# Denominators' token count moved to ScalarE, unit 14's last two sums moved to VectorE, and new orders on all queues

## What is computed

```python
h = layernorm(x)
q, k, v, g = h @ Wq.T, h @ Wk.T, h @ Wv.T, h @ Wg.T       # q, k turned by rotary sin and cos
kv, ksum, vsum = sum_s k v, sum_s k, sum_s v              # per head
num = q kv * scale + vsum
den = q ksum * scale + seq_len                            # seq_len = 256 tokens
x = x + ((num / den + conv(v, lepe_w, lepe_b)) * g) @ Wo.T
y = (fp8(layernorm(x) / s_in) @ fp8(kernel / s_k)) * (s_in * s_k)
out = x + (bf16(y) + bias)
```

## Time and profile before

| | |
|---|---|
| median of three runs | 168.14 us |
| the profiled execution | 168.33 us |
| its span, first to last instruction | 166.5 us |
| mean granted TensorE clock | 0.975 of full speed |
| PE busy | 151.4 us (91%) |
| DVE busy | 149.5 us (90%) |
| ACT busy | 125.9 us (76%) |
| POOL busy | 136.1 us (82%) |

### The profile page before, as it was taken

One profiled execution on the slowest core, in us unless ns is written; L12 is line 12 of the kernel. 1 busy time (PEld: TensorE's weight loads), 2 busy tenths in 40 slices (PEclk: granted clock), 3 DMA queues, 4 the chain that ended last, 5 costly groups with the idle time before them and its releaser, 6 DMA issues.

```text
span 166.5 us, 3690 instructions
## 1 busy us (share of the span) xinstructions
PE 151.4 (91%) x1052; PEld 123.3 (74%) x1052; DVE 149.5 (90%) x281; ACT 125.9 (76%) x342; POOL 136.1 (82%) x164
## 2 busy tenths in 40 slices
PE   7687999999999999999999999999999999987520
PEld 2365898796877889797988888879979787865300
DVE  1269999999899999999999999999999999999563
ACT  3748857566888888989989898798687977672851
POOL 1426986866899999999989899999879989889860
PEclk9999999999999999999999999999999999999955
DMA  4955030222061915065625536263405131514223
GB/s 128 286 145 136 0 67 2 58 43 63 10 150 32 246 27 140 5 150 137 162 65 129 155 95 194 35 159 85 108 7 122 36 74 23 128 33 99 77 61 112
DMA packets 29286, 15.74 MB, mean 95 GB/s; under 512 B 9680, under 2 KB 26960, under 8 KB 29264
## 3 DMA queue, kind: packets, MB, share of 16 engines
q1 hardware_dynamic: 28688, 15.22, 36.8%
q10 hardware_dynamic: 576, 0.26, 0.6%
HBM read 5.25 MB, written 4.19 MB: 57 GB/s over the span
## 4 chain that ended last, share of the span: by engine, by line
PE 78%; DVE 5%; POOL 5%; issue 4%; SPq 3%; DMA 3%; ACT 1%; POOLq 0%; DVEq 0%; ACTq 0%
PE bank L1284 9%; PE bank L1275 8%; PE p_num L1331 8%; PE bank L1294 8%; PE bank L1320 8%; PE p_num L1339 8%; PE bank L1358 7%; PE bank L1302 7%; PE bank L1310 4%; PE bank L1348 4%; PE bank L1267 4%; DMA w_raw<-in_L_attn_Wo_dram 3%; DVE acc L982 2%; PE bank L1400 2%; POOL yc L724 1%
## 5 line engine op out<-in xcount | busy, mean ns | idle before, releaser
L982 DVE SCALAR_TENSOR_TENSOR acc<-bank,conv_w,acc 128x510 f32<-128x510 f32 (+1 forms) x48 | 34.6, 721 | 0.4 <-ACT acc L433 0.2
L394 ACT ACTIVATE h<-xs,nmr,rs 128x128 f32<-128x128 f32 x64 | 26.2, 481 | 1.2 <-POOL nmr L664 1.2
L452 ACT ACTIVATE h<-x,nmr,rs 128x128 bf16<-128x128 f32 x60 | 24.6, 483 | 2.1 <-POOL nmr L675 1.5
L708 POOL TENSOR_TENSOR k<-k_turned 128x512 f32<-128x512 f32 x16 | 20.4, 1274 | 4.2 <-DVE k_turned L967 4.2
L661 POOL TENSOR_TENSOR rs<-ve,minus_half 128x4 f32<-128x4 f32 (+1 forms) x17 | 16.6, 977 | 8.2 <-ACT ve L385 8.2
L717 POOL TENSOR_TENSOR acc<-acc,outer 128x508 f32<-128x508 f32 x16 | 20.3, 1270 | 1.1 <-DVE acc L982 1.1
L672 POOL TENSOR_TENSOR rs<-ve,minus_half 128x4 f32<-128x4 f32 (+1 forms) x17 | 16.6, 975 | 5.7 <-ACT ve L443 5.7
L701 POOL TENSOR_TENSOR qT<-q_turned,q_swapped 128x512 f32<-128x512 f32 x16 | 20.4, 1274 | 0.6 <-DMA q_swapped<-q_turned 0.6
L967 DVE TENSOR_TENSOR k_turned<-bank,turn_k 128x1024 f32<-128x1024 f32 x16 | 19.5, 1222 | 0.8 <-PE bank L1284 0.6
L955 DVE TENSOR_TENSOR q_turned<-bank,turn_q 128x1024 f32<-128x1024 f32 x16 | 19.4, 1214 | 0.0
L1320 PEld LDWEIGHTS bank<-v,k 128*128 128x128 f32 x128 | 16.5, 190 | 3.5 <-issue 3.3
(11 more groups left out here) (90 smaller groups left out, 338.1 us busy)
## 6 DMA issues: line engine op xcount, KB each, us to landing
q_swapped<-q_turned SPq DMA_DIRECT2D x32, 128.0 KB, 2.4
xs<-_attn_hidden_states_dram SPq DMA_DIRECT2D x15, 256.0 KB, 3.7
out_dram<-ob SPq DMA_DIRECT2D x15, 256.0 KB, 2.7
xs<-_attn_hidden_states_dram SPq DMA_DIRECT2D x2, 128.0 KB, 2.7
turn_q<-in_turn_q_dram SPq DMA_DIRECT2D x1, 256.0 KB, 4.0
turn_k<-in_turn_k_dram SPq DMA_DIRECT2D x1, 256.0 KB, 4.3
out_dram<-ob SPq DMA_DIRECT2D x2, 128.0 KB, 1.8
h2T<-h SPq DMA_TRANSPOSE x14, 2.5
```

The source lines that it names most:

```text
L394: last = nc.scalar.activation(h[:, s, t], xs[:, u % NX, t], ACT.Identity, scale=rs1[:, s, t:t + 1], bias=nmr1[:, s, t:t + 1])
L452: last = nc.scalar.activation(h2[:, s3, t], x2[:, u % 4, t], ACT.Identity, scale=rs2[:, s, t:t + 1], bias=nmr2[:, s, t:t + 1])
L708: nc.gpsimd.tensor_tensor(k[:, u % 3], k_turned[:, s, :, :, 0:D // 2], k_turned[:, s, :, :, D // 2:D], ALU.add).then_inc(k_done, 1)
L982: nc.vector.scalar_tensor_tensor(out=part, in0=p_vT[:, :, lo + off:hi + off], scalar=conv_w[:, k:k + 1], in1=part, op0=ALU.mult, op1=ALU.a ...
```

## The change

The addition of the token count to the denominators becomes an activation on ACT (add_tokens, with the count as a bias held in a new tile `tokens`) for units 0 to 14; den gets a second slot; DVE's invert is the reciprocal alone and waits for den. Unit 15 keeps its additions on DVE, in halves. add_bias(14) and final_sum(14) leave POOL and are done by DVE around end_norm2, with semaphores of their own. The PSUM results are placed in other banks, and the call lists of SP, ACT, POOL, DVE and PE are written in a new order throughout, with waits to match the banks. No step of the computation is left out. Cut to its core (loops, start and end of the lists):

```diff
-        den = sb("den", [P, TPU, H])
+        den = sb("den", [P, 2, TPU, H])
+        tokens = sb("tokens", [P, 1])
...
-        p_q = bank[3]
-        p_k = bank[0][:].rearrange("p (t d) -> p t d", t=TPU)
-        p_v = bank[0][:].rearrange("p (t d) -> p t d", t=TPU)
-        p_kv = bank[2][:, 0:BPU * NW].rearrange("p (j e) -> p j e", j=BPU)
-        p_h2T = bank[3][:, 0:W // 2].bitcast(BF16)
-        p_hT = bank[3]
-        p_proj = bank[1][:].rearrange("p (t d) -> p t d", t=TPU)
+        p_q = bank[4]
+        p_k = bank[3][:].rearrange("p (t d) -> p t d", t=TPU)
+        p_v = bank[2][:].rearrange("p (t d) -> p t d", t=TPU)
+        p_kv = bank[4][:, 0:BPU * NW].rearrange("p (j e) -> p j e", j=BPU)
+        p_h2T = bank[2][:, 0:W // 2].bitcast(BF16)
+        p_hT = bank[2]
+        p_proj = bank[5][:].rearrange("p (t d) -> p t d", t=TPU)
         p_gT = bank[1]
-        p_vT = bank[5][:].rearrange("p (j s) -> p j s", j=BPU)
-        p_t1T = bank[4]
-        p_y = bank[0]
-        p_first_hT = [b[:, 0:S] for b in (bank[5], bank[3])]
-        p_end_h2T = [b[:, 0:S // 2].bitcast(BF16) for b in (bank[0], bank[1])]
-        p_end_y = [b[:, 0:S].rearrange("p (t d) -> p t d", t=TPB) for b in (bank[4], bank[3])]
-        p_end_t1T = [b[:, 0:S] for b in (bank[3], bank[2])]
-        p_end_gT = [b[:, 0:S] for b in (bank[4], bank[1])]
-        p_end_proj = [b[:, 0:S].rearrange("p (t d) -> p t d", t=TPB) for b in (bank[4], bank[1])]
+        p_vT = bank[0][:].rearrange("p (j s) -> p j s", j=BPU)
+        p_t1T = bank[5]
+        p_y = bank[5]
+        p_first_hT = [b[:, 0:S] for b in (bank[3], bank[5])]
+        p_end_h2T = [b[:, 0:S // 2].bitcast(BF16) for b in (bank[3], bank[2])]
+        p_end_y = [b[:, 0:S].rearrange("p (t d) -> p t d", t=TPB) for b in (bank[5], bank[4])]
+        p_end_t1T = [b[:, 0:S] for b in (bank[4], bank[5])]
+        p_end_gT = [b[:, 0:S] for b in (bank[3], bank[0])]
+        p_end_proj = [b[:, 0:S].rearrange("p (t d) -> p t d", t=TPB) for b in (bank[1], bank[0])]
 
...
-                sp.wait_ge(ob_done, count(u))
+                if u == LAST - 1:
+                    sp.wait_ge(late_ob_done, 1)
+                else:
+                    sp.wait_ge(ob_done, count(u))
...
             load_x(3)
+            swap_q(0)
             load_x(4)
-            swap_q(0)
+            swap_q(1)
             load_x(5)
-            swap_q(1)
             swap_q(2)
+            load_x(6)
+            swap_q(3)
             turn_h2(0)
-            swap_q(3)
             turn_h2(1)
             swap_q(4)
...
+            def add_tokens(u):
+                act.wait_ge(num_filled, count(u))
+                if u >= 2:
+                    act.wait_ge(rden_done, count(u, 2))
+                nc.scalar.activation(den[:, u % 2], p_num[:, :, D:NW], ACT.Identity,
+                                     bias=tokens[:, 0:1]).then_inc(den_done, 1)
...
+            for t in range(9, 11):
                 norm2(t - 4)
+                var_eps1(t)
                 move_v(t - 1)
-                var_eps1(t)
                 conv_middle(t - 1)
                 conv_outer(t - 1)
                 quantise_if_small(t - 4, is_small)
                 norm1(t)
                 var_eps2(t - 3)
+                add_tokens(t - 2)
                 move_y(t - 4)
                 move_hT(t)
...
             norm2(13)
             var_eps2(14)
+            move_y(12)
+            norm2(14)
             quantise_if_small(13, is_small)
+            quantise_if_small(14, is_small)
+            var_eps2(15, 0)
             move_y(13)
-            norm2(14)
-            var_eps2(15, 0)
-            quantise_if_small(14, is_small)
             var_eps2(15, 1)
             move_y(14)
             end_norm2()
...
+            for t in range(10, 11):
                 pow2(t - 4)
                 add_bias(t - 5)
-                add_q(t - 2)
                 final_sum(t - 5)
                 pow1(t)
+                add_q(t - 2)
+                add_k(t - 1)
                 sum_outer(t - 2)
...
+            pow2(14)
             final_sum(11)
-            pow2(13)
-            add_q(15)
             add_bias(12)
-            sum_outer(15)
             final_sum(12)
-            pow2(14)
+            pow2(15, 0)
+            pow2(15, 1)
             add_bias(13)
             final_sum(13)
-            pow2(15, 0)
-            pow2(15, 1)
-            add_bias(14)
-            final_sum(14)
...
+            def add_bias(u):
+                s = u % 2
+                dve.wait_ge(yb_done, count(u))
+                dve.wait_ge(ob_done, count(u, 2))
+                nc.vector.tensor_tensor(yc[:, s], yb[:, s], fb[:].unsqueeze(1).to_broadcast([P, TPU, D]),
+                                        ALU.add).then_inc(late_yc_done, 1)
+
+            def final_sum(u):
+                dve.wait_ge(late_yc_done, 1)
+                dve.wait_ge(ob_free[u % 3], 16 * (u // 3) + 16)
+                nc.vector.tensor_tensor(ob[:, u % 3], x2[:, u % 4], yc[:, u % 2], ALU.add).then_inc(late_ob_done, 1)
...
+            def add_tokens(u, j=None):
+                part = part_of(j, TPU)
+                dve.wait_ge(num_filled, count_last(u, j=j))
+                nc.vector.tensor_scalar(den[:, u % 2, part], p_num[:, part, D:NW], float(S), None,
+                                        ALU.add).then_inc(den_done, 1)
+
             def invert(u, j=None):
                 part = part_of(j, TPU)
-                dve.wait_ge(num_filled, count_last(u, j=j))
-                nc.vector.tensor_scalar(den[:, part], p_num[:, part, D:NW], float(S), None,
-                                        ALU.add).then_inc(den_done, 1)
                 dve.wait_ge(den_done, count_last(u, j=j))
-                nc.vector.reciprocal(rden[:, part], den[:, part]).then_inc(rden_done, 1)
+                nc.vector.reciprocal(rden[:, part], den[:, u % 2, part]).then_inc(rden_done, 1)
...
+            set_up_qk()
+            set_up_v()
             set_up_g()
-            set_up_v()
-            set_up_qk()
             stats1(1)
-            set_up_o()
-            stats1(2)
             turn_q_unit(0)
             turn_k_unit(0)
-            stats1(3)
+            stats1(2)
+            set_up_o()
             set_up_ffn()
             conv_tap(0, 0)
-            turn_k_unit(1)
+            stats1(3)
             conv_tap(0, 1)
             mask_kv(0)
             conv_tap(0, 2)
+            turn_k_unit(1)
             turn_q_unit(1)
...
+            for t in range(8, 10):
+                stats1(t)
+                add_lepe(t - 3)
+                gate(t - 3)
                 mask_kv(t - 2)
-                add_lepe(t - 3)
-                stats1(t)
-                gate(t - 3)
-                turn_q_unit(t - 1)
                 turn_k_unit(t - 1)
                 quantise_if_wide(t - 4, is_small)
                 residual(t - 3)
                 conv_tap(t - 1, 0)
                 stats2(t - 3)
+                turn_q_unit(t - 1)
                 invert(t - 2)
                 conv_tap(t - 1, 1)
                 divide(t - 2)
...
-            conv_tap(14, 0)
+            conv_tap(14, 2)
+            turn_q_unit(15)
             turn_k_unit(15)
-            mask_kv(14)
-            conv_tap(14, 1)
-            turn_q_unit(15)
-            conv_tap(14, 2)
+            invert(14)
+            divide(14)
+            residual(13)
+            stats2(13)
+            add_lepe(14)
             quantise_if_wide(12, is_small)
-            residual(13)
-            invert(14)
-            stats2(13)
-            divide(14)
             conv_tap(15, 0)
-            mask_kv(15)
-            add_lepe(14)
             gate(14)
             conv_tap(15, 1)
+            mask_kv(15)
             conv_tap(15, 2)
+            residual(14)
             quantise_if_wide(13, is_small)
-            residual(14)
+            stats2(14)
+            add_tokens(15, 0)
             invert(15, 0)
-            stats2(14)
             divide(15, 0)
+            add_tokens(15, 1)
             invert(15, 1)
             divide(15, 1)
             add_lepe(15, 0)
...
+            add_bias(14)
             end_norm2()
+            final_sum(14)
...
+            transpose_h(0, j=1)
             turn_weights()
-            transpose_h(0, j=1)
+            project_q(0)
+            project_k(0, (hT_done, count_first(0, j=0)))
             project_v(0)
+            project_g(0)
             turn_weights_o((v_ready, 1), (g_ready, 1))
-            project_q(0, (hT_done, count_first(0, j=1)))
-            transpose_v(0, (hT_done, count_first(0, j=0)))
-            project_k(0, (v_done, count(0)))
+            transpose_v(0)
             sum_v(0, (qk_ready, 1), (o_ready, 1))
-            project_g(0)
-            transpose_h(1, (q_turned_done, count(0)))
+            transpose_h(1, (v_done, count(0)))
+            key_value(0, (q_turned_done, count(0)))
+            project_v(1, (hT_done, count_first(1)))
```

(67 more changed lines are left out.)

## The result

| | before | after |
|---|---|---|
| median | 168.18 us (4 runs, 168.0 to 168.35) | 169.52 us (4 runs, 169.18 to 169.9) |
| span of the profiled execution | 166.5 us | 167.4 us |
| idle time of TensorE, 57 to 141 us | 0.00 us | 2.16 us |

What follows compares the result with a forecast made beforehand. TensorE was taken as the floor of a loop nearly balanced with DVE. T at 148.65 plus 14.6 us, less 0.2, gave a span of 163.05, 3.45 under 166.5; 168.14 - 3.45 = 164.7 us, range 162.9 to 167.6.

Steps and rivals of the forecast that it cites:

- Part 2: Start of the kernel: TensorE's gaps shrink from 3.1 to 1.2 us, everything later comes 1.9 us earlier (0.5 to 3.0).
- the places named: New TensorE gaps at the start: 0.3 us at sum_v(0), 0.3 at hT(1), 0.25 at project_q(4).
- Part 1: Loop: the denominators' add on ACT relieves DVE, TensorE stays the floor; cost 0 to 1.1 us over nine units.
- rival 2: Loop: the denominators' hand-off through ACT makes DVE the bound; 168.5 to 170 us, chance 0.1.
- Rival 1: Loop: ACT's add comes 0.3 us later than walked and eats part of the gain; 165.8 to 167.4 us, chance 0.2.
- Bank sharing: Loop: new bank sharing adds TensorE waits, each met 1 to 2 us before it is asked for; priced at nothing.
- rival 3: Bank sharing: residual, late by 0.2, holds ffn and transpose_t1, giving back the start's gain; 167.9 to 168.4 us, chance 0.05.
- Part 3: End: stats2(14) ends 3.4 us earlier, then 14.6 us to the span's end instead of 14.4; bounds -1.5 to +1.5.
- T: End of stats2(14) near the kernel's end: 152.06 us before, forecast at 148.65.
- Rival 4: End: POOL holds each of DVE's two unit-14 operations 1.15 us ahead of end_norm2; +1.2 us, 165.9 us, chance 0.1.
- smaller gaps: Loop: 0.2 us taken off the span because small gaps shrink with DVE's 3.2 us of relief.

Runs made afterwards that it cites:

- before with 19 products: The kernel before with TensorE's warm-up cut into 19 products (11 wide, 8 narrow) in place of 13, same columns; 169.76 us, ratio 1.0094.
- the first experiment: The changed kernel with ACT's quantise of units 0 to 13 reading untransposed h2, so not waiting for the transposing DMA; 167.15 us, ratio 0.9939.

## Why the prediction was wrong

**Part 2, the start: right.** 2.03 us ahead at unit 7 (1.8 without the ffn that was put off) for 1.9 forecast, with new gaps of 0.21 and 0.36 us at two of the places named (0.3 and 0.25 forecast) and 0.14 at the third, hT(1) (0.3).

**The step that failed** is the last sentence of Part 2: "q_turned(0) is done at 10.7 and ob, x and h2T loads are asked for units later than they land; nothing for these." For h2T it was false, and it could have been read from the trace of before. There turn_h2 is issued at 69.70, lands 2.5 us later, at 72.2, and the quantise starts at 72.24. No idle time was shown, since ACT came to it at just that moment; the slack was under 0.1 us, not a unit. I had looked for waits, found none before 119 us, and took none for "early". After, ACT reached it at 71.03, 3.3 us behind the issue, which would do for a landing of 2.5 and doesn't for 4.2. That both fetches near 70 and 98 us meet a transposition after and none before is chance, and nothing in the prediction could have told it; that there was no slack to take a late landing could have been told. It was false for ob as well: store(1) behind swap_q(7). Of SP's queue I walked the moves of swap_q(0) and turn_h2(0) only, not those in the middle of its list. Their price in the loop, by the runs: 2.0 us of span for h2T, 0.6 for the store (165.4 and 164.8 us).

**Part 1, the loop.** 0 to 1.1 us was the bound, from ACT's late add. The mechanism of rivals 1 and 2 was seen (DVE idle before its reciprocal, released by ACT, 0.53 and 1.28 us), but it happened twice, not in each unit, and not for the reason given: with the add on DVE again the time is no better. The relief of DVE and ACT's new 0.27 us (forecast 0.27) are worth 0.4 us together at most. The direction came out as in rival 2 and the cause is another one, which none of the rivals had. (Rival 1's upper end is also added wrongly: 164.7 + 2.3 is 167.0, not 167.4.)

**Bank sharing,** priced at nothing, cost 0.3 to 0.43 us at project_o(5), which waits for move_y(3) to leave the bank: ffn(3) was put in ahead of it. That is rival 3's mechanism, at one place of the loop.

**Part 3, the end.** T came 3.75 us late, 3.30 of it already there in attend(14). The rest is transpose_t1(14), which waits 0.42 us for residual(13) (a bank again). From T on it was 15.0 us for 14.6. That end_norm2 would be two long passes beside POOL's yc and ob of unit 13, and that unit 14's yc takes about 0.5 us (0.42 measured), was right. Rival 4 did not happen: DVE's yc had started 0.07 us ahead of POOL's, and it was POOL's that took longer, 1.37 us for 1.15. It had also seen that unit 13's two operations come into the very place that the change clears, and that a free POOL would give 2.3 us; measured, it gives 1.5.

**The sum again.** Forecast span 163.05; 4.35 us were missing. Without the wait for h2T the span goes from 167.4 to 165.4, with store(1) earlier too to 164.8: 2.6 us. In that last kernel attend(14) ends at 141.42 and stats2(14) at 149.76, so that 0.67 us are still lost in the loop (the waits for yb and v), 0.44 from there to T, 0.44 behind T, and the 0.2 that I had taken off for smaller gaps never came: 1.75 us in all. All 4.35 are thus placed.

**What stays open.** Shown are that ACT's wait for h2T costs 2.0 us, that two of the transposition's closing packets pass only when a fetch that came in at the end of its block is over, and that moving the fetch adds or removes such a landing. That these two packets and the fetch lie on the same DMA engine is my reading: their times agree to 0.01 us in after and in before with 19 products, but the views don't name the engine. Why the landing is recorded 1.2 us behind them is open. And it is not the whole rule: 4.6 us with a fetch at 2.5 us, 3.9 with one at 1.0, and the 5.3 amid loads and stores lie outside it. The collision near 70 us was never moved in after. The starts of TensorE's transposes tell roughly what each wait is worth: after is 0.14 us behind the first experiment's kernel at unit 7, 0.60 at unit 10 and 1.86 at unit 11, so that most of it lies at the fetch near 98 us.

## What to carry to other kernels

An operation that shows no wait is not an operation with slack: for each transfer that a change moves, put its landing beside the start of its reader, as 72.2 beside 72.24 here, and do it for the whole of the issuing queue. A long wait on one engine is traced to the first idle entry of the engine that released it: DVE's 1.28 us for den was ACT's 1.21 us for a DMA. And before work is moved off an engine at the end, see what moves into its place: here two sums of unit 14 left POOL for a gain of 1.1 us alone, and two of unit 13 came in and took it.

## What the runs showed of the hardware

- Instructions come in by DMA, here nine packets of 16 KB on a queue of their own in a span, ten where TensorE's program has 21 more products; their times depend, among other things, on that: 28 narrow products for 7 wide ones at the start moved the fetch at 98 us by 1.4 us. A DMA that transposes 128x512 bf16 mostly lands in 2.4 to 2.5 us without such a fetch, and landed in 4.0 to 4.5 in the 16 cases where one came 1.8 to 2.0 us behind its issue; its data were through in time, and two of its closing packets passed when the fetch ended. Six more products in the warm-up made the kernel before 1.6 us slower.
- 16 or 40 idle instructions on TensorE moved neither the time (167.98 and 169.54 us) nor the fetches near 70 and 98 us.
- POOL and DVE hold each other up both ways: end_norm2 2.40 us beside POOL and 0.60 without; and in the kernel with unit 13's sums on DVE, POOL's power of two columns takes 1.24 us while DVE runs a sum of 0.69, where it is 0.70 elsewhere:

```profile
158.10 0.70 POOL L709 TENSOR_TENSOR rs<-ve,minus_half 128x2 f32<-128x2 f32 x1
...
159.03 1.24 POOL L709 TENSOR_TENSOR rs<-ve,minus_half 128x2 f32<-128x2 f32 x1
```
